# Moving work at three seams of a one-core vision tower with a mixture of experts: the first tile of attention, the exponentials of three generators, the last stage

## What is computed

```python
h = embed(patches) + pos; h = concat(cls_tok, h)                  # 32 images x 38 tokens x 256
x = layernorm(h); q, k, v = x@Wq.T, x@Wk.T, x@Wv.T                # 16 heads of 16
q, k = layernorm(q), layernorm(k)                                 # per head
h = h + softmax(causal(q @ k.T)) @ v @ Wo.T + bo
xn = layernorm(layernorm(h)) * gamma + beta; residual = layernorm(h)
abel = gelu(xn @ abel_w + abel_b)
topw, topi = top_k(xn @ gate_w + gate_b, 2); w = softmax(topw)    # 8 experts, 2 per token
moe = sum_k w_k * expert_k(xn)                                    # gelu(xn@ew1+eb1)@ew2+eb2
moe = moe @ expm(gens[0]) @ expm(gens[1]) @ expm(gens[2])         # 256x256 each
g = sigmoid(concat(abel, moe) @ gc_w + gc_b)
out = h + residual + abel*(1-g) + moe*g
```

## Time and profile before

| what | us |
|---|---|
| three runs | 370.74, 372.91 (median), 374.26 |
| profiled execution | 372.73 |
| its span on the core | 370.9 |
| PE busy | 329.2 (89%) |
| DVE busy | 222.3 (60%) |
| ACT busy | 179.2 (48%) |
| POOL busy | 153.4 (41%) |

### The profile page before, as it was taken

The page is one execution under the profiler, slowest core; times in us unless marked ns, Lnnn a source line. Parts: engine busy times, 40 slices in busy tenths (PEclk is TensorE's granted clock), DMA queues, the critical chain, the costliest instruction groups (busy, mean ns, idle before and its releaser), DMA issues.

```text
span 370.9 us, 6801 instructions
## 1 busy us (share of the span) xinstructions
PE 329.2 (89%) x2010; PEld 278.9 (75%) x2010; DVE 222.3 (60%) x598; ACT 179.2 (48%) x422; POOL 153.4 (41%) x169
## 2 busy tenths in 40 slices
PE   2999799949899999987898897999999999995994
PEld 1788454539788888875686786899899988894893
DVE  0225559698989999987798289598312211004275
ACT  1000254487888988954435762243344545550131
POOL 2002624041445664472022374668536687742000
PEclk9999999985999999999999999899999999999699
DMA  7742511123111110029514465245325556532442
GB/s 264 269 148 70 203 58 55 55 81 139 48 48 47 47 46 21 2 71 408 190 38 143 117 201 151 71 129 171 99 87 170 158 185 216 182 115 67 145 140 82
DMA packets 20544, 45.78 MB, mean 123 GB/s; under 512 B 2150, under 2 KB 12836, under 8 KB 20260
## 3 DMA queue, kind: packets, MB, share of 16 engines
q1 hardware_dynamic: 17732, 37.80, 30.6%
q0 software_dynamic: 2496, 6.82, 5.5%
q10 hardware_dynamic: 288, 0.81, 0.7%
HBM read 38.20 MB, written 7.22 MB: 122 GB/s over the span
## 4 chain that ended last, share of the span: by engine, by line
PE 73%; DVE 12%; DMA 5%; ACT 5%; issue 3%; POOL 1%; DVEq 1%; SPq 0%; POOLq 0%; ACTq 0%
PE banks L1467 9%; PE banks L1409 9%; PE banks L1476 9%; PE banks L1222 7%; PE banks L1329 5%; PE banks L1252 5%; PE banks L1305 5%; PE banks L1548 3%; PE banks L1558 3%; PE banks L1347 3%; PE banks L1292 3%; PE banks L1380 2%; PE banks L1257 2%; PE banks L1278 2%; DVE qk_sb L1095 2%
## 5 line engine op out<-in xcount | busy, mean ns | idle before, releaser
L1467 PE MATMUL banks<-qn_sb,w_sb 128*128 128x128 f32 x416 | 51.0, 276 | 1.5 <-ACT qn_sb L641 1.1
L1467 PEld LDWEIGHTS banks<-qn_sb,w_sb 128*128 128x128 f32 x416 | 48.6, 192 | 2.0 <-ACT qn_sb L641 1.4
L1476 PE MATMUL banks<-w_sb,sq_sb 128*128 x208 | 49.6, 383 | 0.0
L641 ACT ACTIVATE qn_sb<-banks,col_sb 128x128 f32<-128x128 f32 x52 | 21.0, 455 | 52.8 <-PE banks L1454 47.8
L1146 DVE TENSOR_TENSOR pT_sb<-banks,p_sb 128x256 f32<-128x256 f32 x26 | 11.0, 425 | 52.8 <-PE banks L1476 44.0
L460 POOL DMA_INDIRECT y_rows<-pT_sb,sidx_sb x26 | 26.0, 999 | 40.3 <-DVE pT_sb L1146 39.0
L1476 PEld LDWEIGHTS banks<-w_sb,sq_sb 128*128 128x128 f32 x208 | 38.9, 193 | 4.9
L652 ACT ACTIVATE sq_sb<-banks,col_sb 128x128 f32<-128x128 f32 x104 | 32.5, 366 | 14.6 <-PE banks L1467 12.7
L1222 PE MATMUL banks<-wtok_sb,patch_sb 128*114 128x256 f32 x132 | 31.5, 405 | 7.0 <-DMA wtok_sb<-in_w_tok 7.0
L454 POOL DMA_INDIRECT qn_sb<-z_rows,gidx_sb x26 | 28.4, 1094 | 18.8 <-PE banks L1454 10.5
L1222 PEld LDWEIGHTS banks<-wtok_sb,patch_sb 128*114 128x114 f32 x132 | 25.3, 192 | 12.8 <-DMA patch_sb<-in_patches 7.0
(11 more groups left out here) (224 smaller groups left out, 660.7 us busy)
## 6 DMA issues: line engine op xcount, KB each, us to landing
w_sb<-in_w SPq DMA_DIRECT2D x26, 512.0 KB
w_sb<-in_w SPq DMA_DIRECT2D x1, 4096.0 KB, 12.7
patch_sb<-in_patches SPq DMA_DIRECT2D x11, 342.0 KB, 3.0
vrep_sb<-v_rows SPq DMA_DIRECT2D x33, 114.0 KB
qk_sb<-y_rows SPq DMA_DIRECT2D x10, 228.0 KB
v_rows<-v_sb SPq DMA_DIRECT2D x11, 114.0 KB
z_rows<-h_sb SPq DMA_DIRECT2D x11, 114.0 KB
out_rows<-h_sb SPq DMA_DIRECT2D x10, 114.0 KB
```

The costliest lines, as they stand in the source:

```text
L1467: last = nc.tensor.matmul(bank[2 + 2 * s + c // 2][:, (c % 2) * 128:(c % 2 + 1) * 128], w1_sb[:, w0:w0 + 128], xsT_sb[:, (2 * s + k) * 128 ...
L1476: last = nc.tensor.matmul(bank[6 + s][:, 0:D], hidT_sb[:, s * HID + k * 128:s * HID + (k + 1) * 128], w2_sb[:, ds(e * 4 * D + k * D, D)], ...
```

## The change

It has four parts.

1. *Embedding's end.* `norm_x` of tiles 0 and 1 stands ahead of the last two adds on DVE; PE waits for all adds before the first matmuls into the shared banks.
2. *Attention's start.* ACT copies tile 0's queries and keys ahead of the second root, DVE copies tile 0's keys and makes its shift ahead of the second refinement, PE makes tile 0's scores ahead of tile 1's keys. The roots move from `p_sb` to `w1_sb`, so that the shift may write `p_sb` earlier. POOL no longer waits for the second roots ahead of tile 2.
3. *Exponentials.* The polynomials move one slot back, the loop two, the gate sums ten. Only generator 0 is squared in a slot. Its transposed form and Y1, Y2 transposed are kept in slots 14, 16 and 18. Behind the last slot stand four products: Y2 squared, Y1 squared in transposed form (Y1 as the stationary operand and Y1 transposed as the moving one), then (I+Y1)(I+Y2), then (I+Y0) times that. The identity enters as a half, added to a copy of Y2 in slot 14.
4. *Last stage.* ACT scales each token's first row by its weight, DVE adds the second row times its weight, PE only transposes the sum. abel is subtracted on PE, by a negative identity, into the same bank; rotations use four banks instead of two. POOL makes one negative identity instead of 22 scaled ones.

```diff
+        def expert_rows(t, k):
+            return qk_sb[0:real(t), (2 * t + k) * D:(2 * t + k + 1) * D]
...
+        minus_sb = patch_sb[:, G * 512:G * 512 + T]
...
-        newton_sb = p_sb[:, 0:2 * NT * 2 * NH]
+        newton_sb = w1_sb[:, 0:2 * NT * 2 * NH]
...
-        P0_AT, P1_AT, MORE_AT, SQ_AT, E_AT = 3, 6, 9, 10, (14, NS)
+        P0_AT, P1_AT, MORE_AT, SQ_AT, E0T_AT, Y1T_AT, Y2T_AT = 4, 7, 11, 12, 14, 16, 18
...
-        LAST_AT = 19
+        GATE_AT = 12
...
-            pool.wait_ge(rs_set, 2)
...
                 if j == NT + 1:
-                    pool.wait_ge(y_set, G)
-                    pool.wait_ge(resid_set, 1)
-                if NT + 1 <= j < 2 * NT + 1:
-                    for a in (2 * (j - NT - 1), 2 * (j - NT - 1) + 1):
-                        pool.tensor_scalar(diag_sb[0:T, a * T:(a + 1) * T], con_sb[0:T, K_ID:K_ID + T],
-                                           wt_sb[0:T, 2 * NT + a:2 * NT + a + 1], None, ALU.mult).then_inc(diag_set, 1)
+                    pool.tensor_scalar(minus_sb[0:T, :], con_sb[0:T, K_ID:K_ID + T], -1.0, None, ALU.mult).then_inc(minus_set, 1)
...
-            for t in range(2):
-                keep_q(t, t)
-                keep_k(t, t, 0)
-                keep_k(t, t, 1)
+            keep_q(0, 0)
+            keep_k(0, 0, 0)
+            keep_k(0, 0, 1)
+            root(1)
+            nc.scalar.activation(al_sb[:, 78:79], con_sb[:, K_ZERO:K_ZERO + 1], ACT.Exp)
+            keep_q(1, 1)
...
+            keep_k(1, 1, 0)
+            keep_k(1, 1, 1)
...
+            def weigh_first(t):
+                act.wait_ge(d_gather[t], 16)
+                nc.scalar.activation(expert_rows(t, 0), expert_rows(t, 0), ACT.Copy,
+                                     scale=wt_sb[0:real(t), 2 * NT + t:2 * NT + t + 1]).then_inc(first_set, 1)
+            act.wait_ge(resid_set, 1)
+            for t in range(3):
+                weigh_first(t)
...
             for t in range(NT):
+                if t + 3 < NT:
+                    weigh_first(t + 3)
...
+            def norm_x(t, s):
+                if isinstance(t, int) and t in (0, 8):
+                    dve.wait_ge(rstd1, 1 + t // 8)
+                nc.vector.tensor_scalar(stage_sb[0:T, s * D:(s + 1) * D], h_sb[0:T, ds(t * D, D)],
+                                        mv_sb[0:T, ds(2 * t, 1)], r1_sb[0:T, ds(t, 1)], ALU.subtract, ALU.mult).then_inc(xh_set, 1)
+            norm_x(0, 0)
+            norm_x(1, 1)
...
-            dve.wait_ge(rstd1, 1)
-            def norm_x(t, s):
-                nc.vector.tensor_scalar(stage_sb[0:T, s * D:(s + 1) * D], h_sb[0:T, ds(t * D, D)],
-                                        mv_sb[0:T, ds(2 * t, 1)], r1_sb[0:T, ds(t, 1)], ALU.subtract, ALU.mult).then_inc(xh_set, 1)
...
+            keep_k(0, 0)
+            shift(0, 0)
+            norm_k(2, 0)
+            keep_k(1, 1)
...
-            keep_k(0, 0)
-            norm_k(2, 0)
-            keep_k(1, 1)
-            shift(0, 0)
...
-            def second():
-                dve.wait_ge(e_made, 1)
-                link(nc.vector.tensor_tensor(Y[0], Y[0], Y[1], ALU.add))
-                nc.vector.tensor_tensor(Y[0], Y[0], bank[0][:, :], ALU.add).then_inc(e_kept, 1)
-                dve.wait_ge(e_kept, 1)
-            def third():
-                link(nc.vector.tensor_tensor(Y[0], Y[0], Y[2], ALU.add))
+            def half_second():
+                dve.wait_ge(e_turned, 1)
+                dve.wait_ge(s_kept_cr, 3 * more + G + 1)
+                link(nc.vector.tensor_copy(Y[0], Y[2]))
...
-                    link(nc.vector.tensor_tensor(diagonal, diagonal, eye, ALU.add))
+                    stt(diagonal, eye, 0.5, diagonal)
+            def rotation():
+                dve.wait_ge(s_made, 3 * more + 2)
+                nc.vector.scalar_tensor_tensor(out=Y[0], in0=Y[0], scalar=2.0, in1=bank[4][:, :], op0=ALU.mult,
+                                               op1=ALU.add).then_inc(s_kept_cr, 1)
+                dve.wait_ge(s_made, 3 * more + 3)
+                nc.vector.scalar_tensor_tensor(out=YT[1], in0=YT[1], scalar=2.0, in1=bank[0][:, :], op0=ALU.mult,
+                                               op1=ALU.add).then_inc(s_kept_cr, 1)
+                dve.wait_ge(s_kept_cr, 3 * more + G + 3)
+                dve.wait_ge(e_made, 1)
+                nc.vector.tensor_tensor(Y[1], Y[0], bank[4][:, :], ALU.add).then_inc(e_kept, 1)
+                weigh_both(0)
+                dve.wait_ge(e_kept, 1)
...
-                link(nc.vector.tensor_tensor(yw3[:, :, 0:D], Y[0].rearrange("p (k d) -> p k d", k=2),
-                                             bank[4][:, :].rearrange("p (k d) -> p k d", k=2), ALU.add))
+                link(nc.vector.tensor_tensor(yw3[:, :, 0:D], Y[1].rearrange("p (k d) -> p k d", k=2),
+                                             bank[5][:, :].rearrange("p (k d) -> p k d", k=2), ALU.add))
...
-                u = j - SQ_AT
-                if 0 <= u < 2:
-                    square(3 * more + u + 1, u, 0)
-                if j == E_AT[0]:
-                    second()
+                if j == SQ_AT:
+                    square(3 * more + 1, 0, 0)
...
-                if 2 <= j < NT + 2:
-                    gate_of(j - 2)
+                if GATE_AT <= j < GATE_AT + NT:
+                    gate_of(j - GATE_AT)
+                if j == E0T_AT:
+                    half_second()
...
-            square(3 * more + 3, 2, 0)
-            dve.wait_ge(s_kept_cr, 3 * more + G + 3)
-            third()
+            def weigh_both(t):
+                dve.wait_ge(first_set, t + 1)
+                nc.vector.scalar_tensor_tensor(out=expert_rows(t, 0), in0=expert_rows(t, 1), scalar=wt_sb[0:real(t), 3 * NT + t:3 * NT + t + 1],
+                                               in1=expert_rows(t, 0), op0=ALU.mult, op1=ALU.add).then_inc(both_set, 1)
...
             def rotated(t):
-                n, s = real(t), t % 2
-                mo, zt = v_sb[0:n, t * D:(t + 1) * D], z_sb[0:n, NT + t:NT + t + 1]
+                n, b = real(t), bank[2 + t % 4]
+                zt = z_sb[0:n, NT + t:NT + t + 1]
...
-                nc.vector.tensor_scalar(zt, bank[2 + s][0:n, D:D + 1], z_sb[0:n, t:t + 1], -87.0, ALU.add, ALU.max).then_inc(z_bounded, 1)
-                nc.vector.tensor_tensor(mo, bank[2 + s][0:n, 0:D], h_sb[0:n, t * D:(t + 1) * D], ALU.subtract).then_inc(rot_kept, 1)
+                nc.vector.tensor_scalar(zt, b[0:n, D:D + 1], z_sb[0:n, t:t + 1], -87.0, ALU.add, ALU.max).then_inc(z_bounded, 1)
+                if t + 3 < NT:
+                    weigh_both(t + 3)
...
-                dve.wait_ge(rot_kept, t + 1)
-                nc.vector.scalar_tensor_tensor(out=h1_sb[0:n, t * D:(t + 1) * D], in0=mo, scalar=g, in1=hb_sb[0:n, t * D:(t + 1) * D],
+                nc.vector.scalar_tensor_tensor(out=h1_sb[0:n, t * D:(t + 1) * D], in0=b[0:n, 0:D], scalar=g, in1=hb_sb[0:n, t * D:(t + 1) * D],
...
+            rotation()
...
+            for t in range(1, 3):
+                weigh_both(t)
...
+            pe.wait_ge(h_added_cr, NT + 2)
...
+            turn_q(0, 0)
...
-            for t in range(2):
-                turn_q(t, t)
-                turn_k(t, t)
+            turn_k(0, 0)
+            turn_q(1, 1)
...
+            turn_k(1, 1)
...
             for j in range(NS):
-                u, e = j - SQ_AT, expert_of(j)
+                e = expert_of(j)
...
-                if 0 <= u < 2:
-                    pe.wait_ge(s_kept_cr, 3 * more + G + u)
-                    turn_square(bank[0], Y[u]).then_inc(s_turned, 1)
-                if j == E_AT[0]:
-                    pe.wait_ge(s_kept_cr, 3 * more + G + 2)
+                if j == SQ_AT:
+                    pe.wait_ge(s_kept_cr, 3 * more + G)
+                    turn_square(bank[0], Y[0]).then_inc(s_turned, 1)
+                if j == E0T_AT:
+                    pe.wait_ge(s_kept_cr, 3 * more + G + 1)
...
-                if j == LAST_AT:
-                    pe.wait_ge(e_kept, 1)
+                if j == Y1T_AT:
+                    pe.wait_ge(e_evac, 1)
+                    turn_square(bank[0], Y[1]).then_inc(s_turned, 1)
+                if j == Y2T_AT:
+                    pe.wait_ge(s_evac, 3 * more + 2)
...
-                if j == LAST_AT + 1:
-                    pe.wait_ge(s_evac, 3 * more + 3)
-                    turn_square(bank[0], Y[0]).then_inc(e_turned, 1)
...
-                if 0 <= u < 2:
-                    pe.wait_ge(s_evac, 3 * more + u + 1)
-                    product(bank[0], YT[u], Y[u]).then_inc(s_made, 1)
-                if j == E_AT[0]:
-                    pe.wait_ge(e_evac, 1)
-                    product(bank[0], YT[0], Y[1]).then_inc(e_made, 1)
+                if j == SQ_AT:
+                    pe.wait_ge(s_evac, 3 * more + 1)
+                    product(bank[0], YT[0], Y[0]).then_inc(s_made, 1)
...
-            pe.wait_ge(e_evac, 2)
-            product(bank[0], YT[2], Y[2]).then_inc(s_made, 1)
```

(29 more changed lines are left out.)

36 lines of the change are left out of this document (14 added, 22 removed).

## The result

The changed kernel took 370.34 us (median of 20 executions, 364.64 to 434.86), the kernel before 372.25 us (20 executions, 369.48 to 439.15). By these medians the change brings 1.9 us, 0.5%. The ratio of 0.9865 (95% interval 0.9821 to 0.9909) is kinder, as it takes only executions within 1.5% of the quickest of their kernel, 8 of the 20 of the changed one and 16 of the 20 of before. The forecast was 361.7 us with a range of 357.5 to 367.5, 11.0 us less than before. The sign was right, and the size was more than twice too large by the ratio (1.35%, some 5 us) and nearly six times by the medians.

A forecast was written before the change was run, and what follows sets the result against it. TensorE was taken to bound the slots and VectorE to pace attention. Gains of 0.6 (front), 8.7 (slots) and 1.7 (behind the slots) sum to 11.0 us: 372.73-11.0 = 361.7 us, range 357.5 to 367.5.

The forecast's parts named there:

- Front: End of embedding and attention's start: VectorE enters attention's loop earlier, gain 0.6 us, bounds -0.4 to 1.3.
- VectorE sets the pace of attention: Attention's loop: TensorE waits for VectorE's copies, so only VectorE's own entry counts; TensorE's 3 to 5 us lead worth nothing.
- Slots: The 26 expert slots on TensorE: terms (a) to (e) sum to a gain of 8.7 us, bounds 4.1 and 9.7.
- (c): Slots: TensorE's stall ahead of the second generator's product goes, 2.61 us, and with it the half clock; together 4.6 us.
- (a): Slots: nine products outside the loop of squarings become seven, two fewer at 1.73 us each, gain 3.46 us.
- (d): Slots: POOL's two scaled identities per slot go, ahead of the row gathers; gain 1.0 us, bounds 0 and 1.5.
- (e): Slots, a cost: with slot 3 bare, slot 4 reaches its gathered rows early and waits, 0.75 us lost.
- Behind the slots: Last products and last stage: rotation starts 0.6 us later, tiles go quicker, gain 1.7 us (2.5 at full clock).
- the first seven tiles go at 1.62 to 1.65, the last three at 1.3 to 1.5: Last stage's us per tile: landings of 1.65 us pace the first seven; last rotation starts at E+27.2, end at E+32.9.
- Rival 4: Slower: thin work and landing waits keep TensorE at 1.2 GHz through all eleven last-stage tiles, 376.9 us; chance 0.03.
- Rival 2: Last stage gives nothing: half clock for 6.8 us or landings pacing everything lose the 1.7, 363.4 us; chance 0.20.
- Rival 1: Slots' stall only moves: late polynomial or waits for gathers in bare slots lose 4.6 us, 366.3 us; chance 0.10.

The follow-up runs named there:

- again: The changed kernel run once more, unaltered, for a second trace: median 370.25 us, ratio 0.986 to the kernel before.
- front_only: The kernel before with parts 1 and 2 alone (end of embedding, start of attention): 378.94 us, ratio 1.010.
- fill_third_tile: The full change with idle matmuls at attention's start and ahead of the slots, plus five ahead of the fourth tile's keys (tile 3): 361.96 us, ratio 0.978.
- before_filled: The kernel before with fourteen idle matmuls, eight at attention's start and six ahead of the slots: 369.32 us, ratio 0.996.
- back_only: The changed kernel without parts 1 and 2: 363.21 us, ratio 0.982 to the kernel before.
- expo_only: The kernel before with part 3 alone, last stage as before with scaled identities: 363.26 us, ratio 0.980.
- filled_old_last_stage: The change without part 2, with idle matmuls through attention's start and ahead of the slots, and the last stage of before (parts 1 and 3): 360.54 us.

## Why the prediction was right or wrong, point by point

The first trace's span is 370.5 us, and the forecast's would have been 370.9-11.0 = 359.9. Of the 10.6 us between, some 6.0 lie ahead of the slots, 4.1 in them and 0.4 behind them.

**Front, 0.6 us forecast: wrong, and the larger part of the miss.** Its first steps came out in part. Queries and keys began at 39.64 (forecast 40.1). VectorE waited for the first scores 3.49 us in the first trace and 2.61 in again (forecast 2.5), with the second half's scores 4.2 and 3.2 in all. It entered the loop at 90.83 and 89.5 (forecast 89.8), which was partly luck, as it had come to its first copies 0.6 to 0.9 us sooner than forecast (73.6 and 73.3 against 74.2). 90.83 is already past the 90.5 that the prediction had named as a sign of being wrong, and front_only entered at 91.37. The step that failed is "VectorE sets the pace of attention, so a lead of TensorE is worth nothing there and only VectorE's own entry counts". It rested on the earlier trace rows, which were taken at 2.4 GHz. At 1.2 GHz TensorE's step is 11.7 to 12.0 us against VectorE's 7.4. One such step is the whole loss: the copies of tile 4 came at 104.57 before and at 109.89 after. From entry to the copies of the last tile it was 58.7 us before (149.04-90.39) and 63.5 after (154.37-90.83). The bound of -0.4 for a fall of the clock was taken from the fall in before, of 10.2 us, which was over at 91.2, as the loop began. I had not asked how long a fall lasts when it reaches into the loop: 6.8 to 30.7 us in these traces.

That idle time makes TensorE's clock fall is shown by the filling. Part 2 sends TensorE through the scores of tile 0 sooner, and then it stands 2.06 and 1.85 us where ScalarE is late, and in the filled traces 2.8 to 3.1 us where VectorE is; with all these waits filled the clock stayed up through attention. The Trainium skill (TensorE: Matmul & The Clock Gate, "HAM oscillation — how this bites in real kernels") describes the same kind of loss, work that starts at 1.2 GHz behind each wait, and the trace agrees: the first scores, behind the wait of 2.06, ran at 0.50. Holding the clock took the full change from 0.995 of before (370.34 to 372.25 us) to 0.976 (361.96 to 371.00), so it was worth 1.9%. But the old order has such waits too (3.4 and 1.9 us in before) and falls behind them. What differs is how far the fall reaches into the loop, to 91.2 in before and to 110.7 in the first trace, and without part 2 it once reached 100.3. Why one fall lasts longer than another stays open.

And with the clock held part 2 still costs 1.7 us by the medians. VectorE enters the loop at 87.34 without it and at 88.77 with it, since in the old order it never waits for first scores but does its second roots meanwhile. This is its first shift behind the first two copies, and the entry, without part 2:

```profile
83.78 0.47 DVE L869 TENSOR_REDUCE mx_sb<-banks 114x8 f32<-114x304 f32 x1
...
87.34 2.36 DVE L857 TENSOR_SCALAR kc_sb<-banks,col_sb 32x152 f32<-32x152 f32 x6
```

Not all of that lead lasts: the copies of tile 4 stand at 101.51 and 102.09, the slots begin at 201.8 and 202.4, only 0.6 apart. The rest of the 1.7 isn't accounted for. In fill_third_tile's trace the slots lost 2.4 us more (124.60 against 122.20) at a wait for gathered rows with 4 us at 1.2 GHz behind it. But two of its executions had a mean clock of 1.00 and took 362.25 and 362.88, so that fall isn't the answer for all of them.

```profile
228.64 0.60 PE L1488 MATMUL banks<-con_sb,qn_sb 128*128 128x128 f32 x2 [1.95 <-DMA qn_sb<-z_rows,gidx_sb]
```

The sum had the wait of 2.5 for scores in it and the 1.3 of part 1, but never asked what part 1 gives alone. By the same rows that would have been 1.3 against 0.6, a sign that part 2 loses.

**Slots, 8.7 us forecast: right at full clock, and a second step failed in the first trace.** At full clock they took 122.69, 122.41 and 122.20 us against 130.69: 8.0 to 8.5. Of that 1.5 us is the clock's, as the old slots took 129.15 with the clock held (before_filled); (c) had it at 2.0. (a) and (c): the earlier trace rows's stall of 2.61 is gone; ahead of the second generator's product TensorE waits not at all in the first trace. (d): 0.7 between two traces for the identities, 1.0 forecast, while slots with the same work differ by up to 0.6. (e), put at 0.75, showed as waits for gathered rows of 0.2 to 1.4 us in most traces, but of 1.53 in back_only and 1.95 in fill_third_tile. In the first trace 10.2 us at 1.2 GHz in the first slots took 3.4 us back (126.09 against 122.69), a fall that the forecast put at nothing: it looked for half clock at the stall and in the last stage only. Part 3 alone was forecast by the same steps at 7.1 us less and gave 7.0.

**Behind the slots, 1.7 us forecast: wrong in kind.** The rotation's start came out: E+11.6 to E+11.8 in all traces of the new stage, forecast 11.5, though the terms that the forecast lists add up to 10.7 only, and nothing names the other 0.8. TensorE's tile came out, 1.50. Two steps failed. First, "the first seven tiles go at 1.62 to 1.65, the last three at 1.3 to 1.5": from the start of the first to the start of the last rotation that is 15.7, measured 16.45 (356.29-339.84 in again), end at E+33.8 instead of E+32.9. The steps there were 1.50 three times, then one of 2.58 with a wait of 0.83 for ScalarE, which stood at a landing, then 1.53 to 1.66 until the last of 1.33. Why that landing came late isn't shown. Second, and more, the end was compared with before's E+35.4, which had 6.8 us at 1.2 GHz in it. With its clock up while TensorE works the old stage ends at E+33.6 (expo_only) and E+33.8 (filled_old_last_stage) too. What the profile seemed to offer here was the clock's, not the work's. In the way of counting that gave 16.45, halving the rows gave 14.8: landings hold the stage, and the forecast's 1.65 us a tile for them was too little for one step.

**The base.** The sum was taken from an execution of 372.73 us. The medians of before were 370.25 to 372.51 later, so up to 2.5 us of a difference from 361.7 may be the base's.

**The rivals.** None of the four came true as put. The chances add up to 1.04, and the 0.04 for a result within 1% of before, which is what the medians gave, was tied to (c) and (d), which held. Rival 4, half clock, had the right mechanism and the wrong place: it looked at the stage whose matmuls were thinned, and the fall came where TensorE was made to run ahead and wait. Rival 2 came nearest in the last stage: landings pace it, and between stages at full clock part 4 gave nothing. Rival 1's wait for gathers in the bare slots was seen in single traces (1.53 and 1.95 us), without its 4.6 us. With the clock held the full change takes 361.96 us, the forecast's 361.7 within its error, but partly by chance: part 1 gave more, and part 2 and part 4 less.

## What to carry to other kernels

A wait on TensorE that costs nothing by the chain of waits can still cost its clock, and a loop paced by another engine at 2.4 GHz may be paced by TensorE at 1.2: work out both paces for every loop that begins behind a seam, and look for TensorE's waits just ahead of such a loop (here 1.85 to 3.4 us). When executions of one kernel fall into groups, read the granted clock of each before any order is blamed. Fill TensorE's idle time with matmuls that nobody reads as a test; here this test was also the remedy. Don't credit a change with the clock of one profiled execution of the kernel before.

## What the runs showed of the hardware that I had not expected

Adding work made a kernel faster: five idle matmuls of some 0.47 us each took 6 to 7 us off. The clock stayed at 1.2 GHz for 23.9 us with TensorE busy 23.19 of them, and for 30.7 us with 29.61; nearly full work did not bring it back at once. The length of a fall changes between executions of one kernel: in the changed kernel 6.8 and 23.9 us in one, 20.5 in another. And filling one place was not enough: with attention's start filled the clock fell in the first slots, with both filled it fell at the wait at tile 3.
